# One gelu over a GpSimd tile and a VectorE tile side by side, in the first attention of an eight-layer kernel

## What is computed

```
disp_win = _windows(disp, delta)
strain = disp_win - disp[:, :, :, None, :]
bond_act = jax.nn.gelu(strain @ W_strain + rel_emb @ W_pos, approximate=False)
bond_logits = (bond_act @ W_bond)[..., 0]
damage_act = jax.nn.gelu(strain @ W_dmg + b_dmg, approximate=False)
damage = jax.nn.sigmoid((damage_act @ W_dmg_out)[..., 0] + b_dmg_out[0])
logits = bond_logits - 10.0 * damage
logits = jnp.where(cmask[None, None], logits, -jnp.inf)
weights = jax.nn.softmax(logits, axis=-1)
out = jnp.einsum('bntd,bntde->bnte', weights, val_win)
```

## Time and profile before

| | |
|---|---|
| median of 3 runs | 2731.39 us (2729.92 to 2732.46) |
| the profiled execution | 2728.21 us, its span 2726.5 us |
| ScalarE busy in the span | 1917.2 us (70%) |
| VectorE busy in the span | 2162.4 us (79%) |
| GpSimd busy in the span | 1030.5 us (38%) |
| the loop over the 256 tiles | from 35.28 us (first gelu) to 553.00 us (last tanh) |

### The profile page before, as it was taken

How to read it: one execution, slowest core, us unless ns; L and a number is a source line. 1 busy time by engine, 2 the same in 40 slices (tenths; PEclk the granted TensorE clock), 3 DMA queues, 4 the chain that set the end, 5 groups by cost and what they waited for, 6 DMA issues and landing times. The chain is left out here.

```text
span 2726.5 us, 46440 instructions
## 1 busy us (share of the span) xinstructions
PE 2275.7 (83%) x19049; PEld 951.1 (35%) x19049; DVE 2162.4 (79%) x2990; ACT 1917.2 (70%) x2053; POOL 1030.5 (38%) x465
## 2 busy tenths in 40 slices
PE   5677777787857777776899989999879889999997
PEld 1122222255322223334333343334534533333334
DVE  6898988868899999976899749997540467899995
ACT  5999999932744344344899849997431379999992
POOL 5999999912069999831000400023100000000000
PEclk8989999979979989988899999999889989999998
DMA  2011111120145545302201110101010130211000
GB/s 81 1 53 56 58 64 50 47 66 1 31 140 177 184 178 178 108 24 74 48 13 33 35 19 4 21 4 50 8 44 0 38 72 17 46 29 26 17 8 25
DMA packets 67021, 145.13 MB, mean 53 GB/s; under 512 B 13639, under 2 KB 30387, under 8 KB 66096
## 3 DMA queue, kind: packets, MB, share of 16 engines
q1 hardware_dynamic: 66800, 142.06, 18.4%
HBM read 117.73 MB, written 24.10 MB: 52 GB/s over the span
## 5 line engine op out<-in xcount | busy, mean ns | idle before, releaser
L2243 ACT ACTIVATE l2x_pT<-ps 128x1024 f32<-128x1024 f32 x512 | 470.3, 1162 | 6.6 <-PE ps L2201 6.6
L2426 ACT ACTIVATE l3he_pT<-ps 128x1024 f32<-128x1024 f32 x480 | 445.0, 1060 | 16.1 <-PE ps L2336 16.1
L798 DVE SCALAR_TENSOR_TENSOR l0a_diff_dve<-l0a_A,l0a_pos,ps 128x512 f32<-128x512 f32 x512 | 344.0, 742 | 1.7 <-PE ps L639 1.3
L1541 PE MATMUL ps<-l1s_hc,all_ident 128*128 128x512 f32 x512 | 264.3, 665 | 90.7 <-POOL l1s_hc L1491 90.7
L1482 POOL TENSOR_TENSOR l1s_dBx<-l1a_dtx,l1a_Bs 128x1024 f32<-128x1024 f32 x128 | 253.3, 2000 | 78.8 <-POOLq L1204 78.8
L2336 PE MATMUL ps<-l3h_Qs,l3h_Ks 75*32 75x512 bf16 x4096 | 272.8, 382 | 12.3 <-DVE ps L2434 11.8
L2201 PE MATMUL ps<-l2m_Qs,l2m_Ks 75*32 75x512 bf16 x4096 | 273.2, 385 | 8.6 <-PEq L2749 8.6
L2216 PE MATMUL ps<-l2x_pT,l2m_Va 128*9 128x512 f32 x2048 | 268.6, 597 | 7.9 <-DVE l2s_oT L2894 2.6
L892 ACT ACTIVATE l0a_diff_pool<-l0a_diff_pool 128x2048 f32<-128x2048 f32 x128 | 243.4, 1901 | 11.8 <-POOL l0a_diff_pool L869 11.5
L2347 PE MATMUL ps<-l3he_pT,l3h_Va 128*9 128x512 f32 x1920 | 250.3, 595 | 1.2
L869 POOL TENSOR_TENSOR l0a_diff_pool<-l0a_A,l0a_a_of_t 128x2048 f32<-128x2048 f32 x64 | 243.3, 3829 | 11.9 <-PE ps L639 11.9
(11 more groups left out here) (505 smaller groups left out, 3760.8 us busy)
## 6 DMA issues: line engine op xcount, KB each, us to landing
l1a_Bs<-l1a_bc SPq DMA_DIRECT2D x64, 512.0 KB, 3.6
l1s_Cs<-l1a_bc SPq DMA_DIRECT2D x64, 512.0 KB, 4.3
l0a_band_rows<-l0a_band SPq DMA_DIRECT2D x32, 512.0 KB, 5.8
l0a_band<-l0a_exps SPq DMA_DIRECT2D x14, 512.0 KB, 5.3
l2m_Ks<-l2m_parts SPq DMA_DIRECT2D x36, 128.0 KB
l2m_Qs<-l2m_parts SPq DMA_DIRECT2D x72, 64.0 KB
l3h_Qs<-l3h_parts SPq DMA_DIRECT2D x72, 64.0 KB
l0a_band<-l0a_zero SPq DMA_DIRECT2D x8, 512.0 KB, 7.4
```

Source lines behind the costliest of these rows:

```text
L798: ins = dve.scalar_tensor_tensor(out[:, c, :], src[:, c, :], pos[:, d:d + 1], bank(1), ALU.add, ALU.subtract)
L1541: mm = pe.matmul(g.ps[:, (4 + 2 * h + q) * CH:(5 + 2 * h + q) * CH], g.ident[:, :], hc[:, m % NHC, q * CH:(q + 1) * CH], start=False, stop ...
L2243: act.activation(pT[:, turn % NPT, :], g.ps[:, slot * QC:(slot + 1) * QC], ACT.Exp).then_inc(expd, 1)
L2426: act.activation(pT[:, (4 * m + j) % NPT, :], g.ps[:, slot(turn)], ACT.Exp).then_inc(expd, 1)
```

## The change

The two rings become one tensor, `diffs`: each of the four ring places holds a GpSimd tile and, right behind it, the VectorE tile of the same pair (2064 elements apart). ScalarE now waits, at even s, for both tiles of the pair and takes them in one gelu of 4096 elements; `gelu_done` counts pairs, and TensorE waits for the pair. The tanh moves from ahead of tile 1 to ahead of tile 2, because tiles 0 and 1 are one instruction. VectorE's, GpSimd's and TensorE's orders stay as they were.

```diff
-        dd = r.sb("diff_dve", [P, ND, 4, CH])
         SLOT = 4 * CH + 16
-        dp = r.sb("diff_pool", [P, NP_ * SLOT])
+        diffs = r.sb("diffs", [P, NP_ * 2 * SLOT + 16])
...
-            if s % TPG in D_AT:
-                return dd[:, i % ND, :, :], diff_dve, i
-            at = i % NP_ * SLOT + (MOVED if moved(s) else 0)
-            return dp[:, at:at + 4 * CH].rearrange("p (c t) -> p c t", c=4), diff_pool, i
+            at = i % NP_ * 2 * SLOT + (MOVED if moved(s) else 0) + (SLOT if s % TPG in D_AT else 0)
+            return diffs[:, at:at + 4 * CH].rearrange("p (c t) -> p c t", c=4), diff_dve if s % TPG in D_AT else diff_pool, i
+
+        def both(s):
+            at = s // 2 % NP_ * 2 * SLOT + (MOVED if moved(s) else 0)
+            return diffs[:, at:at + 2 * SLOT].rearrange("p (k t) -> p k t", k=2)[:, :, 0:4 * CH]
...
-                    pe.wait_ge(gelu_done, s + 1)
+                    pe.wait_ge(gelu_done, s // 2 + 1)
...
-                    if s % TPG == 1 and s > TPG:
+                    if s % TPG == 2 and s > TPG:
                         tanh(s // TPG - 1)
-                    ge, sem, i = slot(s)
-                    act.wait_ge(sem, i + 1)
-                    act.activation(ge, ge, ACT.Gelu).then_inc(gelu_done, 1)
+                    if s % 2 == 0:
+                        act.wait_ge(diff_pool, s // 2 + 1)
+                        act.wait_ge(diff_dve, s // 2 + 1)
+                        act.activation(both(s), both(s), ACT.Gelu).then_inc(gelu_done, 1)
```

## The result

The changed kernel took 2764.01 us (median of 4 runs, 2760.54 to 2767.47) against 2731.93 (4 runs, 2729.92 to 2732.89) for the kernel before on the same chip: the ratio is 1.0112, with an interval of 1.0098 to 1.0126, or 32.1 us. The forecast was 2763.1. The profiled execution took 2763.75 us, 35.5 more than that of before.

A forecast was written before the change was run, and what follows sets the result against it. ScalarE was taken as the bound, GpSimd close behind. Walking tanh to tanh, with ScalarE waiting for VectorE's tiles, put the last tanh 30.0 us later; 1.7 of tail made 31.7: 2731.4 + 31.7 = 2763.1, range 2750 to 2780.

The forecast's parts named there:

- The gelu of 4096: ScalarE's gelu of a pair: lasts 3.61 us, occupies the queue 3.51, instead of 3.60 for two gelus.
- Rival (d): Loss smaller because the merged gelu saves 0.20 us a pair, not 0.10: some 8 us off, 2755; chance 0.10.
- Group 0: First group of a phase: pairs (4,5) and (8,9) wait for VectorE, tanh to tanh 15.81 us instead of 14.61.
- Group 1: Second group: pairs (12,13), (14,15), (16,17) wait for VectorE, then exponentials; next tanh at 23.49 us instead of 19.26.
- the sum: The walk's tanh distances added over all phases, table load ahead of the tanh: 2763.1 us as it stands; chance 0.45.
- rival (b): After the exponentials the table load follows the tanh, saving 1.28 us in phases 1, 3, 5: 2759.3; chance 0.25.
- The order of load and tanh: After group 1's exponentials, the sum put a 1.28 us table load between them and the tanh.
- Group 2 of phases 3 and 5: Tile 23 is late, so pair (22,23) starts at 9.66 us instead of 7.59; next tanh at 16.68.
- Group 3: Last group of a phase: no wait for VectorE, tanh to tanh 14.61 us.
- The end: Behind the last gelu TensorE reduces two tiles, not one: between 0 and 1.8 us more, taken as 1.7.
- (a): ScalarE stays the bound, VectorE's tiles ready when asked: pays 10.1 us plus 2.2 of waits, about 2720; chance 0.08.
- (c): Longer idle times lower TensorE's clock in group 0: 15 to 30 us more, 2778 to 2793; chance 0.12.

The follow-up runs named there:

- the spread order: Changed kernel with logits behind tile 5, maxima and subtractions at tiles 17 to 20, exponentials at 22, displacements at 19 and 25: 2729.66 us, 0.9982.
- the two-gelu form: Changed kernel with each pair taken in two gelus of 2048 back to back, all else kept: 2762.92 us, 1.0107.
- the old gelus in that order: Kernel before, with its gelu per tile and tanh at tile 1, given only the spreading of the spread order: 2732.45 us, 0.9997.

## Why the prediction was right

By its own steps:

- **The gelu of 4096.** Forecast 3.61 long at a pace of 3.51, from the exponentials of 512 and 2048 elements. It lasted 3615 ns on average, and 14.61 for four pairs and a tanh in the spread order gives the pace again. Rival (d), a saving of 0.20 a pair, is out: one against two gelus differs by 0.09.
- **Group 0.** Forecast 15.81 between the tanhs; measured 15.90, in phase 3 and in the other phases alike.
- **Group 1.** The pairs were forecast at 5.38, 10.66 and 15.33 after the tanh; they came at 5.50, 10.78 and 15.45, all 0.12 late: 0.06 is that the logits started 0.76 after the tanh (256.93 less 256.17) and not 0.70, the other 0.06 that ScalarE started 0.09 after a tile's end (261.58 to 261.67) and not 0.03. For the next tanh the sum said 23.49 and rival (b) 22.21: it came at 22.20 (278.37 less 256.17).
- **The order of load and tanh.** This step failed as the sum had it. The rows show exp, tanh, load, gelu. That is the order of rival (b). The Trainium skill, "ScalarE: Activation LUTs", section "Table sets: the hidden batching unit", lists tanh in the set of exp; the trace agrees: no load stands between the exp at 276.56 and the tanh at 278.37. The order's price is as (b) gave it: in phases 2, 4, 6 and 7 the 1.28 only moves into group 2, which has no late tile 23 there (in phase 2, 209.57 to 225.61 is 16.04, against the 14.61 forecast), and in phases 1, 3 and 5 it is a gain, 3.8 in all. (b) with nothing else would have given 2759.3.
- **Group 2 of phases 3 and 5.** Forecast 16.68, the pair (22,23) at 9.66; measured 16.78 and 9.74 (288.11 less 278.37).
- **Group 3.** Forecast 14.61; measured 14.66 in phases 1, 2, 4 and 6, and 15.00 in phases 3 and 5. The step left out the row statistics that VectorE takes at tile 30 (lines 114 and 121, 1.2 us), which made tile 31 late by 0.19 and cost the overlap too. They stand in phase 7 as well (the 0.19 at 579.70), where they make 0.33 before the last tanh.
- **The end.** The tail was sized 1.7. ScalarE's last gelu starts at 579.70, and at the pace the tanh would stand at 583.21; it waited for TensorE until 584.50, 1.29 later, and 0.36 more passed until line 97: 1.65.

The sum's 583.03 for the end of the gelus thus stands against 583.21, but not because every term was right. The first gelu came 1.31 later than before (36.59 against 35.28; it came between 35.3 and 36.8 over all kernels here, changed or not). The table's order takes off 3.84. The remaining 2.7 are terms of under 0.4 each that the walk had left out, nearly all with the same sign: 0.09 in each group 0, 0.10 to 0.15 in each group 2, and in group 3 0.39 twice, 0.33 once and 0.05 four times. The median came within 1 us of the forecast with the help of this cancelling; the mechanism and its terms are good to about 4 us.

**The rivals.** (a) is out: ScalarE waited 35.3 us for VectorE (some 40 were forecast), and tile 5 was ready 0.54 after ScalarE asked for it. What (a) would have needed is shown by the experiments, a different order on VectorE's side; even so none came to its 2720, the lowest median being 2728.67. (c), TensorE's clock, did not occur in the changed kernel where it would have cost: the granted clock was 1.00 through group 0 of each of phases 2 to 7. It did occur in the kernel before with the tanh moved, at some 1.4 us a phase where (c) had 2.5, and nothing in the prediction could tell that the changed kernel would be spared. The windows of the changed kernel (five engine columns, the granted clock third from the end) show the full 2.4 GHz level in group 0 and the 1.2 GHz level behind TensorE's idle times in group 1, where it has little to do:

```profile
250.00:255.00 5.00, 5.00 (x76) 2.77 (x72) 5.00 (x9) 4.79 (x2) 5.00 (x2) 1.00 0.01 3
...
265.00:270.00 5.00, 3.64 (x16) 0.60 (x16) 4.93 (x9) 3.34 (x2) 5.00 (x2) 0.50 0.00 0
```

In that window the reduction of a tile takes 1.82 instead of 1.07, and nothing waits for it: the next tanh follows the exponentials at once.

**What stays open.** What a kernel adds to the stage and what it adds to the median differ by 0.6 to 4.3 us, and by 6.7 for the two-gelu form: between it and the change the stage shows 5.0 us and the median none. Each stage is one trace's. The rest of the program, the same in all of them, took between 2162.2 and 2176.8 us from line 97 on in the profiled executions. The mean granted clock goes along with a part of this: of the twelve executions of the spread kernel, the six with 0.934 or more took 2721 to 2729 us, the six with less 2730 to 2741. Whether it is the cause was not tested.

## What to carry to other kernels

Two neighbouring instructions merged into one save the part of their fixed cost that isn't overlapped, here 0.09 us a pair, and only in stretches in which nothing waits. Before merging, write down for each semaphore how far its producer and its consumer move against each other: here a tanh moved by one gelu of 1.8 us and tiles that are released two at a time cost over three times what the merge could bring, and with the better order the merge brought nothing over the old gelus in that order. A large idle time on an engine isn't room for work if it stands in front of the work that others ask for; where the queues are written by hand, the consumer's move has to be matched on the producer's side, as moving the logits by one tile did for 22 of the 30 us.

## What the runs showed of the hardware

A VectorE copy of 512 fp32 elements took 0.68 us from PSUM each time, but between 0.42 and 3.01 us within SBUF, and the long one shown ended just after GpSimd's tile did. GpSimd's subtraction that began while the copy ran took 1.23 us, against 1.04 for the same line in phases 0 and 1 of that run. The Trainium skill, "SBUF — State Buffer", section "Who interferes with whom", states that a copy in a two-port mode and a GpSimd instruction lock each other out for a whole instruction; the trace agrees as far as it goes, with up to 2.6 us inside one copy (3.01 less 0.42) that the profile books as busy time; in which mode the copy ran no run shows. A tanh directly behind an exp needed no table load (276.56 to 278.37), as it needs none behind a gelu (252.64 to 256.17). TensorE's reduction of a tile took 1.06 or 1.07 us at a granted clock of 1.00 and up to 1.94 at the 1.2 GHz level; behind equal idle times of 2.56 us the clock fell in one phase and not in another.
